# First edge sums of a graph kernel: one-hots two groups ahead among the additions, weighted one-hots that wait piece by piece, four message buffers

## The chip, the cores and the metric

One Trainium2 chip, one NeuronCore. The metric is the device time of one launch, in microseconds (us). The kernel before is timed in three runs, and one further run is profiled. In the rows PE is TensorE's matmul, PEld its weight load, DVE VectorE, ACT ScalarE, POOL GpSimd, SP SyncE; a q behind an engine's name is its instruction queue (register work, reads into registers, DMA issue).

## The reference, cut to what matters

The kernel computes two layers of a graph model over 3125 nodes of 256 features and 50,000 edges that are sorted by destination: layer norm, graph attention, a transformer mixer of four sublayers, a mixture of experts, then a second layer of the same kind. The change touches one step of the first graph attention. Each edge has a message of 64 features and four attention scores; per destination node and head the messages are summed with weight exp(score), the weights themselves are summed, and the edges are counted for the second layer:

```
exp_scores = jnp.exp(scores - scores.max(axis=0, keepdims=True))
sum_exp = jax.ops.segment_sum(exp_scores, dst, num_segments=N)
norm = exp_scores / (sum_exp[dst] + 1e-10)
outs = [jax.ops.segment_sum(messages * norm[:, hd:hd + 1], dst, num_segments=N) for hd in range(H)]
deg = jax.ops.segment_sum(jnp.ones_like(src, dtype=x.dtype), dst, num_segments=n)
```

## The kernel before, in words

The program runs in stages, with a barrier of all engines between two of them (`stage_end`). Stage 2 makes the messages beside the mixer and spills them to HBM (`spill`). Stage 3, the first edge sums, is where the change lies; stage 4 turns the sums (line 1583) and goes on to the experts.

Stage 3 works in 40 groups (`NCG`) of 10 chunks (`CG`) of 128 edges. Two chunks share a window of 48 nodes (`W`), so a group has 5 windows (`PR`). A group goes through the engines so:

- SP loads the group's messages from `spill` into `msg` (lines 826 and 835), one of two buffers, 340 KB; load n waits until PE has ended group n - 2 (`win_ps`). Behind the first two loads it issues the 3 MB of `xin` (line 828).
- DVE makes the one-hots: it compares each edge's node number within the window with an iota (line 3027, `one_hots`) and writes `ohd`, one of two buffers.
- POOL multiplies the one-hots by the weights of three heads in two pieces, of 4 and 6 chunks (line 1054, `weigh_hots`), into `ohx`, one of two buffers. It then writes the column of ones into the messages (line 1040, `ones_column`), and after 25 of the 40 groups adds one tile of `xin` to `z` (line 1065). Before its second weighing POOL waits for all of `xin`. ACT makes the product of the fourth head, chunk by chunk (line 2187).
- PE waits for the column of ones (`msg_one`), sums the degrees from `ohd` (line 1562, bank `pt`), and then for each window multiplies messages by weighted one-hots into one of five banks (line 1565, `pa` and `pb`). A window waits for its weighing piece (`wm_ready`), its ACT products (`ax_ready`), and for DVE to have added the same window of the group before (`win_used`).
- DVE reads the five start positions of the group's windows into registers (line 3033, `window_starts`), then adds each window into `acc` (line 3043) and its degrees (line 3049), `add_windows`. An addition waits for its product and for the addition before it, since windows may overlap.

The order on DVE's queue is written out in the loop: the one-hots of group n + 1, the register read of group n, the five additions of group n.

```
for n in range(NCG):
    if n + 1 < NCG:
        one_hots(n + 1)
    ...
    add_windows(n, window_starts(n))
```

A semaphore that is used up by one stage is used again under another name by a later one; the table `past` (line 595 on) holds the value from which it then counts. `mhalf` is a small constant that POOL's powers use.

Of the kernel before, what the change touches and what calls it, by code (L numbers as in the profile page):

```python
# [25 lines left out]
P = 128  # L26
# [83 lines left out]
MSG_HEAD = 4  # L110
MSG_SLOT = (3, 4, 4, 4, 4)
# [47 lines left out]
def build(nc, ctx, a, out):  # L159
# [44 lines left out]
    hn = sb("hn", [TP, GT, D])  # L204
    s0 = ExitStack()
# [94 lines left out]
    msg = sb("msg", [P, 2, CG, MW], F32, s3)  # L300
# [54 lines left out]
    mhalf = sb("mhalf", [TP, GT], F32, s5)  # L355
# [236 lines left out]
    for new, old, value in (("e_ld0", "wq_ld", 128), ("e_ld1", "bo_ld", 128), ("e_ld2", "wvo_ld", 128), ("e_ld3", "sm_ld", 320),  # L592
# [5 lines left out]
                            ("yo_go", "m_add", 3 * NG * NL), ("uw_ld0", "msg_st0", 16 * NCG), ("uw_ld1", "msg_st1", 16 * NCG), ("uw_ld2", "msg_ld0", 8 * NCG), ("yo_st0", "w1_ld", 48), ("yo_st1", "w2_ld", 64),  # L598
# [114 lines left out]
    def _(sp):  # L713
# [111 lines left out]
        for b in range(2):  # L825
            sp.dma_start(msg[:, b].rearrange("p c f -> p (c f)"), spill[b]).then_inc(s[f"msg_ld{b}"], 16)
# [5 lines left out]
        with sp.Fori(1, NCG // 2) as i:  # L832
            for b in range(2):
                sp.wait_ge(s["win_ps"], (i * 2 + b - 1) * PR)
                sp.dma_start(msg[:, b].rearrange("p c f -> p (c f)"),
                             spill[bass.ds(i * 2 + b, 1)].rearrange("o p c -> p (o c)")).then_inc(s[f"msg_ld{b}"], 16)
# [102 lines left out]
    def _(pool):  # L939
# [97 lines left out]
        def ones_column(n):  # L1037

            pool.wait_ge(s[f"msg_ld{n % 2}"], 16 * (n // 2) + 16)
            nc.gpsimd.memset(msg[:, n % 2, :, MF:MF + 1], 1.0).then_inc(s["msg_one"], 1)  # L1040
# [5 lines left out]
        def weigh_hots(n):  # L1046
# [4 lines left out]
            for at in (slice(0, 4), slice(4, CG)):  # L1051
                cols = slice(n * CG + at.start, n * CG + at.stop)
# [5 lines left out]
        for n in range(NCG):  # L1058
            weigh_hots(n)
            if n >= 2:  # L1060
                ones_column(n)
# [109 lines left out]
    def _(pe):  # L1171
# [377 lines left out]
        for n in range(NCG):  # L1549
            b = n % 2  # L1550
            pe.wait_ge(s["msg_one"], n + 1)
            for q in range(PR):
# [11 lines left out]
                for c in (2 * q, 2 * q + 1):  # L1564
                    last = nc.tensor.matmul(wbank[q][0:MF + 1, 0:MH * W], msg[:, b, c, 0:MF + 1],
                                            ohx[:, b, c].rearrange("p k w -> p (k w)"), start=c == 2 * q, stop=c == 2 * q + 1)
# [388 lines left out]
    def _(act):  # L1955
# [226 lines left out]
        for n in range(NCG):  # L2182
            b = n % 2
            act.wait_ge(s["oh_ready"], n + 1)
            for q in range(PR):
                for c in (2 * q, 2 * q + 1):
# [201 lines left out]
    def _(dve):  # L2388
# [648 lines left out]
        def add_windows(n, starts):  # L3037

            for q, at in enumerate(starts):
# [9 lines left out]
                nc.vector.tensor_tensor(degrees, degrees, pt[0:MF + 1, n % 2, q * W:(q + 1) * W], ALU.add).then_inc(s["deg_used"], 1)  # L3049

        me.link(dve, nc.vector.tensor_copy(ohd_one[:, :], ones[:, 0:MF + 1]))
        one_hots(0)
        for n in range(NCG):
            if n + 1 < NCG:
                one_hots(n + 1)
# [671 lines left out]
```

## Time and profile before

| | us |
|---|---|
| median of three runs (lowest to highest) | 2686.23 (2679.67 to 2689.53) |
| the profiled execution's own time | 2686.39 |
| span of the profiled execution | 2684.7 |
| stage 3, first one-hots to last addition | 1256.0 to 1431.2 |
| mean granted TensorE clock over the span | 0.937 |

The span goes from the first to the last instruction; the own time has some 1.7 us more around it. A row of a timeline has the start in us, the duration in us, the engine, the line and the operation, what is written and what it is made from, and in square brackets the idle time before it with what ended it. Merged rows have a count (x12), and their duration runs from the first start to the last end. A row of one line's instructions has durations in ns as lowest/median/highest, and then the start of the first and of the last.

### The profile page before, as it was taken

How to read it: one execution, taken by the hardware profiler on the slowest of the kernel's cores; microseconds unless marked ns; L12 is line 12 of the kernel's file. 1: busy time of each engine (PE TensorE's matmuls, PEld its weight loads, DVE VectorE, ACT ScalarE, POOL GpSimd, SP SyncE). 2: the span in 40 equal slices, each digit the busy share in tenths (PEclk: the TensorE clock that was granted, in tenths of full speed). 3: DMA queues.
4: the chain of work that ended last, by engine and by line, in shares of the span. 5: the costliest groups of instructions: out<-in, count | busy, mean ns of one | idle time of the engine just before them, and what ended most of it. 6: DMA issues, size and time to landing. Idle time of an engine off the chain costs nothing. (4 is left out here: it accounts for less than half of the span.)

```text
span 2684.7 us, 46904 instructions
## 1 busy us (share of the span) xinstructions
PE 2418.1 (90%) x16106; PEld 2259.9 (84%) x16106; DVE 1758.2 (65%) x4475; ACT 1353.8 (50%) x2913; POOL 1239.0 (46%) x1402
## 2 busy tenths in 40 slices
PE   7888999899988998997999699966888999999998
PEld 6778998799988997997778588855777899998998
DVE  6666777678768776765776523246876677677565
ACT  4334655555545664555553222233333366665687
POOL 1323454244515552565886222245777377776000
PEclk9989999999999999999996699977999599999899
DMA  5211112111121111124233354536666077775011
GB/s 115 71 40 39 39 42 64 45 41 41 44 66 38 43 47 49 44 58 103 84 90 98 98 170 143 142 116 178 196 202 189 14 213 206 218 216 174 24 36 32
DMA packets 150287, 259.77 MB, mean 97 GB/s; under 512 B 35713, under 2 KB 95884, under 8 KB 149926
## 3 DMA queue, kind: packets, MB, share of 16 engines
q0 software_dynamic: 49632, 145.61, 20.5%
q1 hardware_dynamic: 100422, 111.17, 13.9%
q8 instruction: 132, 2.16, 0.3%
q14 instruction: 101, 0.83, 0.1%
HBM read 219.88 MB, written 36.82 MB: 96 GB/s over the span
## 5 line engine op out<-in xcount | busy, mean ns | idle before, releaser
L976 POOL DMA_INDIRECT gat<-table,srcT x400 | 413.0, 1032 | 351.8 <-DVE m L2829 228.8
L1131 POOL DMA_INDIRECT x_rows<-table,srcT x392 | 397.3, 1014 | 184.1 <-issue 120.6
L633 PE MATMUL pa<-w,act 128*125 128x256 f32 x2400 | 357.9, 287 | 13.1 <-DVE act L2588 12.9
L633 PE MATMUL pb<-hT,w 128*128 128x378 f32 (+1 forms) x1920 | 335.8, 311 | 1.8 <-DVE hT L2664 1.0
L633 PEld LDWEIGHTS pa<-w,act 128*125 128x125 f32 x2400 | 313.4, 187 | 17.9 <-DVE act L2588 17.9
L633 PEld LDWEIGHTS pb<-hT,w 128*128 128x128 f32 x1920 | 286.4, 189 | 4.1 <-DVE hT L2664 1.8
L2287 ACT ACTIVATE gf<-pb,bne 128x378 f32<-128x378 f32 (+1 forms) x320 | 194.2, 607 | 157.6 <-PE pb L633 145.7
L2588 DVE TENSOR_TENSOR act<-gf,act 128x378 fp32r<-128x378 f32 (+1 forms) x320 | 153.9, 484 | 106.8 <-ACT act L2005 105.0
L2002 ACT ACTIVATE gf<-pb,b1s 128x378 f32<-128x378 f32 (+1 forms) x320 | 165.9, 518 | 107.8 <-PE pb L633 97.0
L633 PE MATMUL pb<-xT,fw 128*128 128x378 f32 (+1 forms) x960 | 158.8, 316 | 0.0
L2220 ACT ACTIVATE hid<-pb,b1u 128x256 f32<-128x256 f32 x128 | 60.7, 474 | 187.8 <-PE pb L1651 187.8
L2005 ACT ACTIVATE act<-gf 128x378 fp32r<-128x378 f32 (+1 forms) x320 | 149.8, 468 | 10.2
L3570 DVE TENSOR_TENSOR act<-gf,act 128x378 fp32r<-128x378 f32 (+1 forms) x180 | 87.9, 489 | 101.5 <-ACT act L2291 101.0
L633 PE MATMUL pb<-act,fw 128*128 128x378 f32 (+1 forms) x960 | 153.8, 309 | 0.0
L1097 POOL DMA_INDIRECT xtok<-table,tabi x64 | 61.4, 960 | 193.1 <-PE pt L1640 142.7
L633 PEld LDWEIGHTS pb<-xT,fw 128*128 128x128 f32 x960 | 146.2, 196 | 1.4 <-issue 1.3
L633 PEld LDWEIGHTS pb<-act,fw 128*128 128x128 f32 x960 | 142.1, 190 | 0.0
L1651 PE MATMUL pb<-xtT,e 128*128 128x256 f32 x512 | 133.6, 384 | 3.8 <-issue 2.2
L2187 ACT ACTIVATE ohx<-ohd,ex 128x48 f32<-128x48 f32 x400 | 94.4, 320 | 74.5 <-DVE ohd L3027 74.5
L1739 PE MATMUL pg<-x_rows,oh 128*125 128x256 f32 x632 | 105.4, 294 | 28.5 <-DMA x_rows<-table,srcT 18.5
L1054 POOL TENSOR_TENSOR ohx<-ohd,ex 128x576 f32<-128x576 f32 x80 | 110.3, 1399 | 40.1 <-DVE ohd L3027 29.0
L1739 PEld LDWEIGHTS pg<-x_rows,oh 128*125 128x125 f32 x632 | 86.6, 190 | 40.1 <-DMA x_rows<-table,srcT 18.9
(517 smaller groups left out, 5676.4 us busy)
## 6 DMA issues: line engine op xcount, KB each, us to landing
e<-in_L_ffn_W_dram SPq DMA_DIRECT2D x40, 512.0 KB, 4.4
spill<-m SPq DMA_DIRECT2D x80, 170.0 KB
msg<-spill SPq DMA_DIRECT2D x40, 340.0 KB, 2.9
yslots<-yo SPq DMA_DIRECT2D x64, 128.0 KB, 2.0
fraw<-in_L_ffn_W_dram SPq DMA_DIRECT2D x32, 256.0 KB
w1r<-in_L_mix_W_dram SPq DMA_DIRECT2D x7, 1024.0 KB, 4.9
gat<-table,srcT POOLq DMA_INDIRECT x400
x_rows<-table,srcT POOLq DMA_INDIRECT x392, 3.8
```

The lines of the kernel that those rows point to most:

```text
L633: mm = nc.tensor.matmul(ps, lhs(l), rhs(r), start=first and n == 0, stop=last and n == 2)
L976: pool.indirect_dma_start(out=gat[:, i % 2, c, :], out_offset=None, in_=table0, in_offset=bass.IndirectOffsetOnAxis(ap=srcT[:, i * GC + c: ...
L1054: nc.gpsimd.tensor_tensor(ohx[:, n % 2, at, 0:MH - 1, :], ohd[:, n % 2, at, :].bitcast(F32).unsqueeze(2).to_broadcast([P, k, MH - 1, W]), ...
L1131: pool.indirect_dma_start(out=x_rows[:, n % UB, c, :].bitcast(F32), out_offset=None, in_=table1, in_offset=bass.IndirectOffsetOnAxis(ap=sr ...
L1651: last = nc.tensor.matmul(pb[:, f % 2, 0:UT], e1[:, u % 3, k, f * P:(f + 1) * P], xtT[:, u % 2, k, :], start=k == 0, stop=k == H - 1)
L1739: last = nc.tensor.matmul(to, oh1[:, n % UB, c, :], x_rows[:, n % UB, c, k * D:(k + 1) * D], start=c == 0 and k == 0, stop=c == UG - 1 and ...
L2002: nc.scalar.activation(gf[:, f % 2, 0:n], pb[:, f % 2, 0:n], func, bias=bias, scale=scale).then_inc(s["gf_done"], 1)
L2005: nc.scalar.activation(act_[0][:, f % 4, 0:n], gf[:, f % 2, 0:n], ACT.Copy).then_inc(s["f_hi"], 1)
L2187: last = nc.scalar.mul(ohx[:, b, c, MH - 1, :], ohd[:, b, c, :].bitcast(F32), ex[:, n * CG + c, MH - 1:MH])
L2287: nc.scalar.activation(gf[:, f % 2, 0:n], pb[:, f % 2, 0:n], func, bias=bias, scale=scale).then_inc(s["gf_done"], 1)
L2588: nc.vector.tensor_tensor(act_[1][:, f % 4, 0:n], gf[:, f % 2, 0:n], act_[0][:, f % 4, 0:n], ALU.subtract).then_inc(s["f_lo"], 1)
L3570: nc.vector.tensor_tensor(to[1][:, f, 0:n], gf[:, f, 0:n], to[0][:, f, 0:n], ALU.subtract).then_inc(s["f_lo"], 1)
```

## The change

It makes the one-hots of groups 0 and 1 ahead of the loop, and those of group n + 2 inside `add_windows(n)`, behind the second of the five additions, after two waits on POOL's and ACT's work of groups up to n. The weighing pieces on POOL and the ACT products of group n wait for PE's products of group n - 2, which read the same `ohx` buffer: the first piece for two windows, the second for all five, ACT window by window. `msg` has four buffers in place of two; load n waits for the end of group n - 4, and POOL writes the column of ones of group n + 2 behind its weighing of group n. The four first message loads stand ahead of `xin` in SP's queue. `mhalf` leaves the memory that the larger `msg` takes. The numbers of semaphores that are used again follow.

```diff
--- before.py
+++ after.py
@@ -108,6 +108,7 @@
 PAIRS = ((0, 2), (2, 1), (3, 2))
 RING = (0, 1, 2, 0, 1)
 MSG_HEAD = 4
+MSG_RING = 4
 MSG_SLOT = (3, 4, 4, 4, 4)
 UC = 2
 UG = RR
@@ -202,6 +203,7 @@
     si = sb("si", [P, 2 * NT], I32)
     r7 = sb("r7", [TP, 3, NT])
     hn = sb("hn", [TP, GT, D])
+    mhalf = sb("mhalf", [TP, GT])
     s0 = ExitStack()
     bns = sb("bns", [P, NE, 4, H], F32, s0)
     bne = sb("bne", [P, 2, 4, H], F32, s0)
@@ -297,7 +299,7 @@
     s3 = ExitStack()
     xin = sb("xin", [TP, NT, D], F32, s3)
     ex = sb("ex", [P, NCH, MH], F32, s3)
-    msg = sb("msg", [P, 2, CG, MW], F32, s3)
+    msg = sb("msg", [P, MSG_RING, CG, MW], F32, s3)
     ohx = sb("ohx", [P, 2, CG, MH, W], F32, s3)
     ohd = sb("ohd", [P, 2, CG, W], R32, s3)
     ohd_one = sb("ohd_one", [P, MF + 1], R32, s3)
@@ -352,7 +354,6 @@
     cr = sb("cr", [P, H], F32, s5)
     qm = sb("qm", [TP, GT * AH], F32, s5)
     qr = sb("qr", [TP, GT * AH], F32, s5)
-    mhalf = sb("mhalf", [TP, GT], F32, s5)
     n_bn, h_bn = [sb(f"{k}_bn", [TP, GT, 6], F32, s5) for k in "nh"]
     n_mv, h_mv = [sb(f"{k}_mv", [TP, GT, 2], F32, s5) for k in "nh"]
     n_ve, h_ve = [sb(f"{k}_ve", [TP, GT], F32, s5) for k in "nh"]
@@ -595,7 +596,8 @@
                             ("z_add", "tn_T", NL), ("z_ve", "cx_ps", NL), ("z_nr", "cx_go", NL), ("hot_w", "bq_ps", NL), ("b1_go", "bq_ev", NL), ("deg_used", "mo_ps", NL),
                             ("tab_go", "tn_go", NL), ("acc1_0", "ta_go", NL), ("xg_ld0", "gat0", 16 * GC * NCG), ("xg_ld1", "gat1", 16 * GC * NCG),
                             ("xg_T", "n_T", 3 * NG * NL), ("xg_up", "n_hi", 3 * NG * NL),
-                            ("yo_go", "m_add", 3 * NG * NL), ("uw_ld0", "msg_st0", 16 * NCG), ("uw_ld1", "msg_st1", 16 * NCG), ("uw_ld2", "msg_ld0", 8 * NCG), ("yo_st0", "w1_ld", 48), ("yo_st1", "w2_ld", 64),
+                            ("yo_go", "m_add", 3 * NG * NL), ("uw_ld0", "msg_st0", 16 * NCG), ("uw_ld1", "msg_st1", 16 * NCG), ("uw_ld2", "msg_ld0", 4 * NCG), ("msg_ld2", "w1_ld", 48), ("msg_ld3", "w2_ld", 64),
+                            ("yo_st0", "w1_ld", 48 + 4 * NCG), ("yo_st1", "w2_ld", 64 + 4 * NCG),
                             ("rw5", "gat0", 16 * GC * NCG + 16 * NUN), ("rw6", "gat1", 16 * GC * NCG + 16 * NUN), ("ch_used", "bc_ps", NL * NG),
                             ("cg_ld0", "rw0", 0), ("cg_ld1", "rw1", 0), ("cg_ld2", "rw2", 0), ("cg_ld3", "rw3", 0),
                             ("cg_used", "d_add", GT * NL * NG), ("tr_hi", "q_hi", 3 * NG * NL)):
@@ -822,18 +824,18 @@
             sp.wait_ge(s[f"msg_st{b}"], 16 * NCG)
         stage_end(sp, 2)
 
-        for b in range(2):
+        for b in range(MSG_RING):
             sp.dma_start(msg[:, b].rearrange("p c f -> p (c f)"), spill[b]).then_inc(s[f"msg_ld{b}"], 16)
         for to, of in by_rows(xin[:, :, :], a["x"].rearrange("(t p) d -> p t d", p=TP)):
             sp.dma_start(to, of).then_inc(s["xin_ld"], 16)
         sp.dma_start(gw6[:, :, :], a["L0_ffn_gate_w"].rearrange("(h p) e -> p h e", p=P)).then_inc(s["p6_ld"], 16)
         sp.dma_start(lgb6[:, :], a["L0_ffn_gate_b"].rearrange("(o e) -> o e", o=1).to_broadcast([TP, NE])).then_inc(s["p6_ld"], 16)
 
-        with sp.Fori(1, NCG // 2) as i:
-            for b in range(2):
-                sp.wait_ge(s["win_ps"], (i * 2 + b - 1) * PR)
+        with sp.Fori(1, NCG // MSG_RING) as i:
+            for b in range(MSG_RING):
+                sp.wait_ge(s["win_ps"], (i * MSG_RING + (b - MSG_RING + 1)) * PR)
                 sp.dma_start(msg[:, b].rearrange("p c f -> p (c f)"),
-                             spill[bass.ds(i * 2 + b, 1)].rearrange("o p c -> p (o c)")).then_inc(s[f"msg_ld{b}"], 16)
+                             spill[bass.ds(i * MSG_RING + b, 1)].rearrange("o p c -> p (o c)")).then_inc(s[f"msg_ld{b}"], 16)
         with sp.If(rest_flag(sp) == 1):
             sp.wait_ge(s["win_ps"], NPR)
             with sp.Fori(0, NCG) as n:
@@ -1036,8 +1038,9 @@
 
         def ones_column(n):
 
-            pool.wait_ge(s[f"msg_ld{n % 2}"], 16 * (n // 2) + 16)
-            nc.gpsimd.memset(msg[:, n % 2, :, MF:MF + 1], 1.0).then_inc(s["msg_one"], 1)
+            b = n % MSG_RING
+            pool.wait_ge(s[f"msg_ld{b}"], past.get(f"msg_ld{b}", 0) + 16 * (n // MSG_RING + 1))
+            nc.gpsimd.memset(msg[:, b, :, MF:MF + 1], 1.0).then_inc(s["msg_one"], 1)
 
         nc.gpsimd.memset(acc[:, 0:2, :], 0.0).then_inc(s["const"], 1)
         ones_column(0)
@@ -1049,6 +1052,8 @@
                 pool.wait_ge(s["act_go"], 1 + MH)
             pool.wait_ge(s["oh_ready"], n + 1)
             for at in (slice(0, 4), slice(4, CG)):
+                if n >= 2:
+                    pool.wait_ge(s["win_ps"], (n - 2) * PR + at.stop // 2)
                 cols = slice(n * CG + at.start, n * CG + at.stop)
                 k = at.stop - at.start
                 nc.gpsimd.tensor_tensor(ohx[:, n % 2, at, 0:MH - 1, :], ohd[:, n % 2, at, :].bitcast(F32).unsqueeze(2).to_broadcast([P, k, MH - 1, W]),
@@ -1057,8 +1062,8 @@
 
         for n in range(NCG):
             weigh_hots(n)
-            if n >= 2:
-                ones_column(n)
+            if n + 2 < NCG:
+                ones_column(n + 2)
             if n == 0:
                 pool.wait_ge(s["xin_ld"], 32)
             for t in range(n * NT // NCG, (n + 1) * NT // NCG):
@@ -1562,7 +1567,7 @@
                         nc.tensor.matmul(pt[0:MF + 1, b, 0:PR * W].rearrange("p (q w) -> p q w", q=PR), ohd_one[:, :], hots[:, :, k, :],
                                          start=k == 0, stop=k == 1)
                 for c in (2 * q, 2 * q + 1):
-                    last = nc.tensor.matmul(wbank[q][0:MF + 1, 0:MH * W], msg[:, b, c, 0:MF + 1],
+                    last = nc.tensor.matmul(wbank[q][0:MF + 1, 0:MH * W], msg[:, n % MSG_RING, c, 0:MF + 1],
                                             ohx[:, b, c].rearrange("p k w -> p (k w)"), start=c == 2 * q, stop=c == 2 * q + 1)
                 last.then_inc(s["win_ps"], 1)
         with pe.If(rest_flag(pe) == 1):
@@ -2183,6 +2188,8 @@
             b = n % 2
             act.wait_ge(s["oh_ready"], n + 1)
             for q in range(PR):
+                if n >= 2:
+                    act.wait_ge(s["win_ps"], (n - 2) * PR + q + 1)
                 for c in (2 * q, 2 * q + 1):
                     last = nc.scalar.mul(ohx[:, b, c, MH - 1, :], ohd[:, b, c, :].bitcast(F32), ex[:, n * CG + c, MH - 1:MH])
                 last.then_inc(s["ax_ready"], 1)
@@ -3047,12 +3054,15 @@
                     dve.wait_ge(s["deg_used"], past["deg_used"] + n * PR + q)
                 degrees = acc[:, MH:MH + 1, bass.ds(at, W)].rearrange("p o n -> p (o n)")
                 nc.vector.tensor_tensor(degrees, degrees, pt[0:MF + 1, n % 2, q * W:(q + 1) * W], ALU.add).then_inc(s["deg_used"], 1)
+                if q == 1 and n + 2 < NCG:
+                    dve.wait_ge(s["wm_ready"], 2 * (n + 1))
+                    dve.wait_ge(s["ax_ready"], (n + 1) * PR)
+                    one_hots(n + 2)
 
         me.link(dve, nc.vector.tensor_copy(ohd_one[:, :], ones[:, 0:MF + 1]))
         one_hots(0)
+        one_hots(1)
         for n in range(NCG):
-            if n + 1 < NCG:
-                one_hots(n + 1)
             if n == 0:
                 me.link(dve, nc.vector.memset(acc[:, 2:MH, :], 0.0))
                 dve.wait_ge(s["const"], 4)
```

## Rows read from the trace of the kernel before

**Rows 1.** The page: busy time and share of the span, instructions, of each engine.

```profile
PE 2418.1 (90%) x16106; PEld 2259.9 (84%) x16106; DVE 1758.2 (65%) x4475; ACT 1353.8 (50%) x2913; POOL 1239.0 (46%) x1402
```

**Rows 2.** Busy time of each engine in the stage's steady part, then clock, DMA share, GB/s.

```profile
1280.00:1431.00 151.00, 138.22 (x826) 108.33 (x824) 111.41 (x415) 87.24 (x370) 122.00 (x141) 1.00 0.30 86
```

**Rows 3.** Timeline of one group, DVE.

```profile
1342.62 0.35 DVE L3043 TENSOR_TENSOR acc<-acc,pb 65x192 f32 x1
...
1342.89 0.19 DVE L3049 TENSOR_TENSOR acc<-acc,pt 65x48 f32 x1
...
1343.01 0.65 DVE L3027 TENSOR_TENSOR ohd<-iota,relT 128x480 fp32r<-128x480 f32 x1
...
1344.23 0.35 DVE L3043 TENSOR_TENSOR acc<-acc,pa 65x192 f32 x1 [0.57 <-PE pa L1565]
...
1344.79 0.35 DVE L3043 TENSOR_TENSOR acc<-acc,pa 65x192 f32 x1
...
1346.58 0.35 DVE L3043 TENSOR_TENSOR acc<-acc,pb 65x192 f32 x1 [0.18 <-PE pb L1565]
```

**Rows 4.** Timeline of the same group, weight loads and POOL.

```profile
1341.01 1.64 POOL L1054 TENSOR_TENSOR ohx<-ohd,ex 128x864 f32<-128x864 f32 x1
...
1342.75 0.19 PEld L1562 LDWEIGHTS pt<-ohd,ohd_one 128*65 128x65 f32 x2 [0.73 <-POOL msg L1040]
...
1343.73 2.75 POOL L1054 TENSOR_TENSOR ohx<-ohd,ex 128x576 f32<-128x576 f32 x2 [1.03 <-DVE ohd L3027]
...
1344.82 1.27 PEld L1565 LDWEIGHTS pb<-ohx,msg 128*65 128x65 f32 x8
...
1346.49 0.72 POOL L1065 TENSOR_TENSOR z<-z,xin 125x256 f32<-125x256 f32 x1
...
1346.59 0.19 PEld L1562 LDWEIGHTS pt<-ohd,ohd_one 128*65 128x65 f32 x2 [0.50 <-POOL msg L1040]
```

**Rows 5.** The comparison's line, and the register read's line twice, four groups each.

```profile
L3027 DVE TENSOR_TENSOR ohd<-iota,relT x37: 645/648/993, 1279.1 to 1423.0; 128x480 fp32r<-128x480 f32 x37
...
L3033 DVEq TENSOR_LOAD <-base_i x4: 593/1184/1187, 1334.9 to 1346.8; - x4
...
L3033 DVEq TENSOR_LOAD <-base_i x4: 597/1180/1190, 1350.6 to 1362.9; - x4
```

**Rows 6.** Timelines of DVE and POOL at two places where both are busy.

```profile
1299.06 1.43 POOL L1065 TENSOR_TENSOR z<-z,xin 125x256 f32<-125x256 f32 x1
...
1350.56 0.73 POOL L1065 TENSOR_TENSOR z<-z,xin 125x256 f32<-125x256 f32 x1
...
1350.81 0.99 DVE L3027 TENSOR_TENSOR ohd<-iota,relT 128x480 fp32r<-128x480 f32 x1
```

**Rows 7.** Start and end of the stage: one stretch's busy time and GB/s, then timelines.

```profile
1256.00:1266.00 10.00, 4.88 (x29) 3.79 (x28) 7.55 (x7) 5.75 (x22) 3.09 (x4) 0.96 1.11 241
...
1251.34 6.55 SPq L828 DMA_DIRECT2D xin<-in_x_dram  x2
...
1262.27 0.38 SPq L835 DMA_DIRECT2D msg<-spill  x1
...
1271.02 2.75 POOL L1054 TENSOR_TENSOR ohx<-ohd,ex 128x576 f32<-128x576 f32 x2 [11.16 <-DMA xin<-in_x_dram]
...
1275.62 0.35 DVE L3043 TENSOR_TENSOR acc<-acc,pa 65x192 f32 x1 [0.81 <-PE pa L1565]
...
1280.46 0.35 DVE L3043 TENSOR_TENSOR acc<-acc,pa 65x192 f32 x1 [0.69 <-PE pa L1565]
...
1428.01 0.35 DVE L3043 TENSOR_TENSOR acc<-acc,pa 65x192 f32 x1 [1.10 <-PE pa L1565]
...
1430.75 0.35 DVE L3043 TENSOR_TENSOR acc<-acc,pb 65x192 f32 x1 [0.54 <-PE pb L1565]
```

**Rows 8.** The message loads' landing times, and one column of ones that waited for one.

```profile
DMA to landing us min/median/max: 2.7/2.9/4.2
...
1299.00 0.12 POOL L1040 MEMSET msg<- 128x10 f32 x1 [0.46 <-DMA msg<-spill]
```

## The prediction, as recorded before the run

> **What bounds the kernel now.** I read the page first: TensorE is busy for nine tenths of the span [rows 1]. That average hides the stage that the change touches: the forty groups of the first edge sums run from 1256 to 1431 us, 175 us or 6.5% of the span. The busy time by stretch shows their steady part [rows 2], where no engine is full: PE 92%, POOL 81%, DVE 74%. Nothing else of the program changes its work, so the answer lies in those 175 us.
>
> The one-hot comparisons, one a group, give the pace: 37 of them from 1279.1 to 1423.0 us, 36 periods of 4.00 us [rows 5]. What sets it is a loop over two groups, read from the timeline of one group [rows 3, 4]. PE starts group n at 1342.75 and DVE begins to add its fifth window at 1346.58: 3.83 us. From a fifth addition to the comparison of the group after next is 0.39 (1342.62 to 1343.01), from there to the weighing on POOL 0.72, the two weighing pieces take 2.75, and PE starts 0.11 after them, once POOL has written the column of ones. 7.80 us for two groups is 3.90 each; some groups add a POOL or PE delay, and 4.00 is measured. PE itself would allow less: its loads of a group begin at 1342.75 and end at 1344.82 + 1.27 = 1346.09, 3.34 us. This gap of 0.66 us a group, 26 us over the stage, is the most that the change can win.
>
> The other row to see is DVE's own chain. From a fifth addition (1342.62) to the next group's first (1344.23) are 1.61 us. Most of that is not the comparison but the read of the five window starts into registers, which DVE's queue does before it can issue the first addition: 1.18 us in three groups of four, 0.59 in the fourth [rows 5]. The comparison of 0.65 us runs inside this read. Additions then follow each other by 0.56 (1344.23 to 1344.79). So DVE alone needs 1.61 + 4 x 0.557 = 3.84 us with a long read and 3.25 with a short one: it is only just inside the 4.00.
>
> **The change part by part.**
>
> *One-hots two groups ahead, among the additions.* The loop above falls: a group's comparison no longer waits for the fifth addition and its weighing has over a group's time to spare. In the code the comparison now stands behind the second addition, while the register read stays where it was, alone. Its cover is gone. A comparison there costs DVE: 0.27 from an addition to its degree addition (1342.62 to 1342.89), 0.12 to the comparison (to 1343.01), then 0.65 less the 0.08 by which neighbours on DVE overlap (0.35 - 0.27), so 0.96 from the second to the third addition in place of 0.56. That is 0.40 us a group, exposed. The two waits ahead of it (weights and ScalarE's products of the group before) ask for work finished a group earlier, and cost at most a slot in the queue. No row shows a comparison between additions: the lower bound is 0, if it slid into slack as under the read now; the upper is its whole 0.65. I take 0.40, by the overlap in the neighbouring rows. A group is then 1.61 + 3 x 0.557 + 0.96 = 4.24 us with a long read, 3.65 with a short one.
>
> *Does PE still hold DVE up?* It has five banks and can be five windows ahead; 3.34 is below 3.65, so it gets ahead and waits for banks. Every addition then finds its product done, and I count 0.56 for each.
>
> *Weighings that wait piece by piece.* POOL waits for the products of the group two before (two of them, then all five), ScalarE pair by pair. With PE ahead of DVE these are done before the comparison is even made. POOL starts 0.72 after the comparison starts, ends the weighings at 3.47, and in 25 of 40 groups adds z until 3.48 + 0.72 = 4.20.
>
> *That addition against the comparison.* At 1350.56 POOL added z for 0.73 us; the comparison that began at 1350.81 took 0.99 in place of 0.65, and ended as if it had started at 1351.15, 0.14 before the z record's end. The other way round, the z addition at 1299.06, over which a comparison ran, took 1.43 [rows 6]. One waits for the other. So DVE's next comparison can't start before 4.20 - 0.13 = 4.07. A long period (4.24) clears this; a short one (3.65) is held by 0.42 where z is added, in 4 of the 9 short groups: 1.7 us.
>
> The Trainium skill, "SBUF — State Buffer", section "SBUF: two separate sides", states that a DVE operation with two SBUF inputs and a GpSimd operation that reads SBUF take a shared port pair as a lock for the whole instruction. The rows agree; by their times, the lock goes 0.14 us before the end that the record shows. Held to the record's very end it would add 0.13 in those four groups, 0.5 us.
>
> *Four message buffers.* The column of ones is written a group and more ahead, so PE no longer waits for it. A later load is issued when PE ends the group four before and lands in 2.9 us [rows 8]; POOL wants it some 4.5 us after that. It costs nothing. But two more loads of 340 KB now stand ahead of xin in SP's queue, and POOL's second weighing waits for xin: 11.16 us idle until 1271.02 [rows 7]. At the 241 GB/s of that stretch 0.68 MB are 2.8 us; one load of 0.34 MB, issued at 1262.27 and so in competition with the later part of xin, is no longer there, at most 1.4 back. Bounds 1.4 and 2.8; I take 1.8, as that load shared most of the tail.
>
> *Start, worked out.* Weighing 1 runs from 1272.8 to 1275.6, z to 1276.3, weighing 2 to 1279.1. Comparison 3 is asked for 0.39 after group 1's second addition (1275.62 + 1.8), at 1277.8, falls on the longer weighing piece and waits until 1279.0. The fifth addition of group 1 comes at 1279.0 + 0.57 + 2 x 0.56 = 1280.7, group 2's first at 1282.3 to 1282.4, in place of 1280.46 [rows 7]: +1.9.
>
> *mhalf* moves to another address and does the same work. No wait hangs on it: 0.
>
> **Sum.** Group 2's first addition to group 39's: before 1428.01 - 1280.46 = 147.55 us. After: 37 periods, 28 long and 9 short, 28 x 4.24 + 9 x 3.65 = 151.6, less 0.4 for group 38, which makes no comparison, plus 1.7 for the lock: 152.9, +5.3. Last group: four steps of 0.56 in place of 2.74 (1428.01 to 1430.75), -0.5. With the start (+1.9): +6.7. The profiled execution took 2686.4 us (its span 2684.7), so 2693.1; the median of the runs, 0.2 lower, gives 2692.9: I predict 2693.0. The expected gain is given back by DVE, which becomes the bound.
>
> **Rivals.** (a) *PE becomes the bound*: the period falls to 3.34, and 37 x 0.65 = 24 us go; with start and end 2663.6. It needs both the register read and the comparison to leave DVE's path. Against it: the read occupies the queue that must issue the additions, and each addition waits for the one before. 0.12. (b) *The comparison costs DVE nothing*: 0.40 x 36 = 14.4 less, 2678.6. PE and POOL would allow it. Against it: DVE has no idle time left there. 0.10. (c) *Slower, by POOL*: if PE doesn't get ahead, it ends a group only as DVE adds its fifth window, 1.5 us after the comparison's start; the load that waits for this lands at 4.5, POOL's column of ones, due at 3.4, is held, and the z addition behind it runs to 5.3 and locks out the comparison until 5.2. One us in each of 23 groups: 2716. It decides once POOL's z addition is over 0.17 us late; some 0.5 late makes +7, enough to be slower. For it: one memset waited 0.46 for its load even now [rows 8]. Against it: PE's 3.34. 0.18. Against the weighing piece of 1.64 us [rows 4] the comparison could be held in the same way; that needs POOL to be 0.9 us late (4.24 less 3.47, plus 0.13). The Trainium skill's rule on the port pair, named above, states no exception for such a pair.
>
> **How the numbers follow.** What a measurement of this kernel can tell from no change is about 0.5%, 13.4 us. The forecast has 0.60; its own range, comparison 0.2 to 0.6 exposed (-7, +7) and the start, is 2685 to 2702, and 0.08 of it lies above 2699.6. (b) is nearly all within, (a) is faster, (c) slower. Faster 0.14, same 0.60, slower 0.26. The range takes in (b) and the lower half of (c): 2670 to 2708.
>
> **What would show it.** Right: the register reads still take 1.18 and 0.59 us and now stand without a comparison behind them; second to third addition 0.96; fifth to first 1.6; additions never wait for PE; ScalarE and POOL idle for DVE's comparison; PE idle for a DVE bank; comparisons 4.1 apart. Wrong: a period below 3.7 (the read was not on the path), comparisons of over 1 us in many groups (the lock, case c), or PE at the lower clock in mid-stage.

## The result, and the profile after

| | before | after |
|---|---|---|
| median of the runs beside each other, us | 2683.23 (20 runs, 2678.08 to 2693.08) | 2697.84 (20 runs, 2683.67 to 2702.66) |
| ratio, 95% interval | | 1.0037 (1.0026 to 1.0049) |
| profiled execution: time, span, us | 2686.4, 2684.7 | 2700.5, 2698.7 |
| mean granted clock | 0.937 | 0.928 |
| the stage, first comparison to last addition's end, us | 1256.02 to 1431.21: 175.19 | 1257.02 to 1440.36: 183.34 |
| first comparison to group 2's first addition, us | 24.44 | 26.82 |
| group 2's first addition to group 39's, us (per group) | 147.54 (3.99) | 153.82 (4.16) |
| group 39's first addition to its fifth, us | 2.74 | 2.23 |

The ratio makes 9.9 us (7 to 13) of 2683: slightly slower, by less than the 0.5% that the prediction counts as a change. The two medians lie further apart, by 14.6, the means of the 20 runs by 10.5 (2684.5 and 2695.1). The runs of each kernel scatter by 15 to 19, so I hold the parts against the ratio. The stage grew by 8.15 us, which lies inside that interval: 2.4 at the start, 6.3 in the steady part, 0.5 back in the last group. The stage's times come from one profiled execution of each kernel. A second one of the changed kernel, on another chip (e9 below), has 182.32 in place of 183.34: 0.7 less at the start, 0.3 less in the steady part.

The page of the changed kernel, each engine's busy time, share and instructions, beside [rows 1]:

```profile
PE 2423.6 (90%) x16106; PEld 2263.7 (84%) x16106; DVE 1755.6 (65%) x4475; ACT 1352.5 (50%) x2913; POOL 1239.5 (46%) x1402
```

The same work, and sums that moved by 6 us at most: the page doesn't show the change. Nor does the busy time by stretch of the steady part (stretch, length, then PE, PEld, DVE, ACT, POOL, granted clock, DMA share, GB/s), beside [rows 2]:

```profile
1280.00:1435.00 155.00, 138.63 (x828) 108.55 (x827) 107.04 (x408) 87.42 (x370) 120.83 (x139) 1.00 0.28 80
```

DVE is shown busy for 107.04 of 155.00 us, 69%, less than PE and POOL, and yet it sets the pace. One has to read the timeline of its groups. Here are groups 17 and 18 (start, duration, engine, line, operation, tiles; in brackets the idle time before it and what ended it):

```profile
1346.26 0.35 DVE L3050 TENSOR_TENSOR acc<-acc,pa 65x192 f32 x1 [1.11 <-PE pb L1570]
1346.53 0.19 DVE L3056 TENSOR_TENSOR acc<-acc,pt 65x48 f32 x1
1346.81 0.35 DVE L3050 TENSOR_TENSOR acc<-acc,pa 65x192 f32 x1
1347.08 0.19 DVE L3056 TENSOR_TENSOR acc<-acc,pt 65x48 f32 x1
1347.20 0.65 DVE L3034 TENSOR_TENSOR ohd<-iota,relT 128x480 fp32r<-128x480 f32 x1
1347.77 0.34 DVE L3050 TENSOR_TENSOR acc<-acc,pa 65x192 f32 x1
...
1348.88 0.35 DVE L3050 TENSOR_TENSOR acc<-acc,pb 65x192 f32 x1
...
1350.45 0.35 DVE L3050 TENSOR_TENSOR acc<-acc,pa 65x192 f32 x1 [1.11 <-PE pb L1570]
```

From the second addition to the third are 0.96 us, with the comparison between them; from the fifth to the next group's first 1.57. The idle time of 1.11 is put down to PE's product, but that is not what ended it. It is the register read, which the profile keeps on DVE's queue. The waits of 1290 to 1435 us (engine, line, waited for: us in total, times, longest) and the two lines, read and comparison (duration in ns min/median/max, first and last start), over the whole stage:

```profile
ACT ohx L2194 <- DVE ohd L3034: 63.0, 35, 2.2
...
POOL ohx L1059 <- DVE ohd L3034: 32.0, 35, 1.8
...
PE pt L1567 <- DVE acc L3056: 15.3, 26, 0.9
```
```profile
L3040 DVEq TENSOR_LOAD <-base_i x40: 590/1182/1200, 1265.0 to 1436.3; - x40
...
L3034 DVE TENSOR_TENSOR ohd<-iota,relT x40: 647/648/1716, 1257.0 to 1430.5; 128x480 fp32r<-128x480 f32 x40
```

ACT and POOL wait for the comparison, and PE waits for DVE to free a bank, where it used to wait for POOL [rows 4]: all three are now held by DVE. The same in the timelines of PE and POOL around group 18:

```profile
1351.05 0.41 PE L1567 MATMUL pt<-ohd,ohd_one 128*65 128x240 f32 x2 [0.54 <-DVE acc L3056]
```
```profile
1347.93 2.75 POOL L1059 TENSOR_TENSOR ohx<-ohd,ex 128x576 f32<-128x576 f32 x2 [1.39 <-DVE ohd L3034]
1350.62 0.12 POOL L1043 MEMSET msg<- 128x10 f32 x1
1350.67 0.72 POOL L1070 TENSOR_TENSOR z<-z,xin 125x256 f32<-125x256 f32 x1
```

**The start.** xin stands behind two more loads:

```profile
1253.28 8.43 SPq L830 DMA_DIRECT2D xin<-in_x_dram  x2
...
1274.38 2.75 POOL L1059 TENSOR_TENSOR ohx<-ohd,ex 128x576 f32<-128x576 f32 x2 [13.47 <-DMA xin<-in_x_dram]
...
1279.36 1.72 DVE L3034 TENSOR_TENSOR ohd<-iota,relT 128x480 fp32r<-128x480 f32 x1
...
1283.84 0.35 DVE L3050 TENSOR_TENSOR acc<-acc,pa 65x192 f32 x1 [1.11 <-PE pa L1570]
```

From the first comparison to POOL's release by xin were 15.00 us (1271.02 less 1256.02) and are 17.36. Comparison 3 falls on a weighing piece and takes 1.72. How far the start varies from execution to execution is seen in the table below: with four loads ahead of xin it takes 25.99 to 28.68 us (after, e1 to e4, e9, e11), with two 23.44 to 24.77 (before, e7, e8). The longer start is clear of this scatter, its size of 2.4 is not fixed to better than 1 us.

**Behind the stage.** From the last addition's end to the first transposition were 1.09 us and are 1.50. The granted clock fell from the higher of its two levels to the lower near there in both kernels: before, 3.0 us behind the last addition (at 1434.2), after, 1.2 behind it (at 1441.6). The first transpositions, before and after, in the columns of the stretch above:

```profile
1432.25:1433.70 1.45, 1.40 (x13) 1.40 (x13) 0.43 (x4) 0.00 (x0) 0.00 (x0) 1.00 0.12 33
```
```profile
1441.80:1443.40 1.60, 1.54 (x8) 1.54 (x8) 0.08 (x1) 0.00 (x0) 0.00 (x0) 0.50 0.31 35
```

Before, 13 of them still ran at clock 1.00 (2.4 GHz); after, all eight of that stretch ran at 0.50 (1.2 GHz). The trace of after runs 9.15 us behind that of before at the last addition's end (1.00 from ahead of the stage, 8.15 from it) and 10.8 behind by the sixteenth transposition. These 1.6 us did not last. Some 130 us later the same products ran at the lower level before and at the higher one after:

```profile
1565.00:1567.00 2.00, 2.00 (x6) 1.55 (x6) 0.85 (x2) 0.03 (x1) 0.00 (x0) 0.50 0.75 280
```
```profile
1575.00:1577.00 2.00, 2.00 (x11) 1.77 (x10) 0.85 (x2) 0.47 (x1) 0.00 (x0) 1.00 0.91 322
```

Behind them the traces lie 8.4 apart, less than at the stage's end. The spans end 14.0 apart, so the rest came in later stages, in two executions of kernels whose runs scatter by 15 to 19. What the traces show of the change for certain is the stage's 8.15; the 9.9 of the ratio, with 7 to 13, agrees with that and needs nothing more.

### The profile page after: what moved, and what is told of

It reads as the page before. It is cut to its first block and busy times, and to the rows that moved or that the text cites. A ratio compares the mean times of both kernels' runs of the same rounds, so it can differ in the third digit from the quotient of the medians.

```text
span 2698.7 us, 46992 instructions
## 1 busy us (share of the span) xinstructions
PE 2423.6 (90%) x16106; PEld 2263.7 (84%) x16106; DVE 1755.6 (65%) x4475; ACT 1352.5 (50%) x2913; POOL 1239.5 (46%) x1402
```

## The experiments

All ratios are against the kernel before on the same chip. e1 to e4 and e5 to e8 ran on two chips on which it takes 2809 and 2810 us, e9 and e10, then e11 and e12, on two where it takes 2688 and 2689. Of the difference some 17 us lie ahead of the stage and some 97 behind it (e1's trace against that of after). The stage's own times agree where a kernel ran on both kinds of chip (e6 151.45, e12 151.63), so I compare those. Each is from one profiled execution. "Steady" is group 2's first addition to group 39's; "start" the first comparison to group 2's first addition.

| kernel | whole, us | ratio (95%) | stage | start | steady (pace) |
|---|---|---|---|---|---|
| before | 2683.23 | | 175.19 | 24.44 | 147.54 (3.99) |
| after | 2697.84 | 1.0037 | 183.34 | 26.82 | 153.82 (4.16) |
| e1 comparison under the read | 2805.87 | 0.9999 (0.9974 to 1.0025) | 171.79 | 27.26 | 141.84 (3.83) |
| e2 short reads | 2805.07 | 1.0008 (0.9984 to 1.0032) | 169.57 | 26.27 | 140.60 (3.80) |
| e3 both | 2802.86 | 0.9993 (0.9963 to 1.0023) | 163.01 | 25.99 | 134.18 (3.63) |
| e4 both, no z | 2771.6 | one run | 159.42 | 28.46 | 128.00 (3.46) |
| e5 both, z late | 2792.55 | 0.9940 (0.9919 to 0.9961) | 156.51 | 15.99 | 137.67 (3.72) |
| e6 both, z late on DVE | 2787.87 | 0.9923 (0.9896 to 0.9950) | 151.45 | 15.95 | 132.80 (3.59) |
| e7 xin first | 2822.0 | one run | 180.74 | 24.77 | 153.27 (4.14) |
| e8 before, short reads | 2811.36 | one run | 174.07 | 23.44 | 147.30 (3.98) |
| e9 = after again | 2703.92 | one run | 182.32 | 26.10 | 153.52 (4.15) |
| e10 after, z late | 2686.75 | 1.0003 (0.9983 to 1.0024) | 175.16 | 17.50 | 154.96 (4.19) |
| e11 reads twice | 2742.95 | one run | 221.92 | 28.68 | 190.55 (5.15) |
| e12 = e6 | 2665.39 | 0.9910 (0.9888 to 0.9932) | 151.63 | 16.05 | 132.89 (3.59) |

**e1: the comparison back under the read.** In the changed kernel, the comparison behind the fifth addition:

```diff
-                if q == 1 and n + 2 < NCG:
+                if q == PR - 1 and n + 2 < NCG:
```

> The changed kernel with one edit: the one-hots of group n + 2 stand behind the fifth addition, so ahead of the next register read, and no longer behind the second. Theory (DVE's queue sets the pace, and the comparison costs 0.40 us because it lost the read as its cover): second to third addition 0.56 in place of 0.96, fifth to first still 1.57 to 1.61 with a long read. DVE alone would then allow 3.84 (long) and 3.25 (short), 3.70 on average; POOL and the comparison, which wait for each other, need 4.07 in groups with a z addition and 3.35 in the others, 3.80 on average, so some 3.8 a group against 4.16 measured: 12 to 14 us less than the changed kernel, 2 to 4 less than the kernel before. Rival (the pace of the changed kernel comes from the waits piece by piece or from the lock, not from where the comparison stands): the place makes no difference, within 3 us of the changed kernel.

The steady part is 12.0 us shorter than after (12 to 14 were expected), the stage 11.6. DVE's timeline from a fifth addition:

```profile
1356.99 0.35 DVE L3050 TENSOR_TENSOR acc<-acc,pb 65x192 f32 x1
1357.26 0.20 DVE L3056 TENSOR_TENSOR acc<-acc,pt 65x48 f32 x1
1357.38 0.68 DVE L3034 TENSOR_TENSOR ohd<-iota,relT 128x480 fp32r<-128x480 f32 x1
1358.67 0.35 DVE L3050 TENSOR_TENSOR acc<-acc,pa 65x192 f32 x1 [0.61 <-PE pa L1570]
```

Fifth to first is 1.68, 0.11 more than after: the read starts 0.28 behind the fifth addition, where it was 0.17, and in the queue the comparison's waits now stand ahead of it. Against it stand the 0.40 of the comparison that is no longer exposed. Groups take 3.91 with a long read, 3.32 with a short one. So the place of the comparison is what turns a gain into a loss: with it under the read the same change shortens the stage by 3.4 us. Over the whole kernel so little can't be seen (ratio 0.9999).

**e2: short reads.** The window starts are copied once into rows of eight, and each group reads from there:

```diff
+    base_8 = sb("base_8", [1, NCG * 8], I32, s3)
+        me.link(dve, nc.vector.tensor_copy(base_8[:, :].rearrange("o (n k) -> o n k", k=8)[:, :, 0:PR],
+                                           base_i[:, :].rearrange("o (n k) -> o n k", k=PR)))
-                base_i[0:1, n * PR:(n + 1) * PR], engines=[mybir.EngineType.DVE]
+                base_8[0:1, n * 8:n * 8 + PR], engines=[mybir.EngineType.DVE]
```

> The changed kernel with the window starts copied once into rows of eight, so that each group's five lie at a multiple of 32 bytes. Theory (the register read is on DVE's path, and is long where its start is not at a multiple of 16 bytes): all 40 reads take 0.59 us, fifth to first addition 0.98 in every group. DVE's period falls to 3.60; where POOL adds z the comparison is held until 4.07, in 25 of 40 groups, so 3.89 on average: some 10 us less than the changed kernel, and comparisons of 1.1 us in the z groups. Rival 1 (the read is hidden by something else): no change. Rival 2 (the lock does not hold DVE in general): 3.60, 20 us less.

The read's line, in the form of the one above:

```profile
L3041 DVEq TENSOR_LOAD <-base x38: 584/587/591, 1300.5 to 1441.1; - x38
```

Every read is short, fifth to first is 0.98 in all groups but two (1.33), and the steady part is 13.2 us shorter than after, more than the 10 expected. Part of what the read gave is taken by POOL's work, which holds the comparison: from group 2 on 21 of 36 comparisons take 0.79 us or more. Eleven are held by a z addition, and the worst of those make a group of 4.07, which is the bound that the prediction gave for this; ten are held by a weighing, for 0.2 us, mostly in groups of 3.82. Unheld groups take 3.60. The expectation had 25 groups at 4.07 and so too small a gain.

**e8: short reads in the kernel before.** The counterpart, which a theory of the read alone would have faster:

> The kernel before with short register reads alone. Theory (before the change a loop over two groups set the pace, PE's products, the comparison, POOL's weighings, and the read lay beside it): the pace stays at 3.9 to 4.0 us a group, at most 3 us less over the stage. Rival (the read was on the path before too): 0.4 to 0.6 less a group, 15 to 20 us.

Its steady part is 147.30 in place of 147.54. The same 0.6 us that are worth 0.36 a group after are worth nothing before: DVE's chain did not set the pace there. That fits the two-group loop.

**e11: reads used twice.** In the changed kernel each group reads its five values twice, and the second set places the degree additions:

```diff
-            add_windows(n, window_starts(n))
+            add_windows(n, window_starts(n), window_starts(n))
```

> The changed kernel with a second register read per group, whose values place the degree additions, so that both reads are needed (the kernel with a read whose values nothing used had 40 reads in its trace, as many as the changed kernel: it was the changed kernel again). Theory (the read is serial on DVE's queue): fifth to first addition 1.57 + 1.18 = 2.75 with a long read, 0.98 + 0.59 = 1.57 with a short one; 38 us more from group 2 to group 39 than the 154 of the changed kernel, less up to 2 where the longer group frees the comparison from the lock. Rival (part of it overlaps with waiting that would be there anyway): less than 25 us more.

```profile
L3040 DVEq TENSOR_LOAD <-base_i x8: 595/1181/1192, 1351.5 to 1368.1; - x8
...
1351.34 0.35 DVE L3050 TENSOR_TENSOR acc<-acc,pb 65x192 f32 x1
...
1354.12 0.35 DVE L3050 TENSOR_TENSOR acc<-acc,pa 65x192 f32 x1 [2.32 <-issue]
```

The steady part grows by 36.7 us. Fifth to first is 2.79 in a long group (2.78 in the one shown, over 3.1 in two), and 1.60 in a short one. The read is on the path in full.

**e9** was to show the same with a second read whose values nothing used. Only 40 reads stood in its trace, so it was the changed kernel again and tells nothing of the read. It does repeat the changed kernel on another chip: stage 182.32, pace 4.15.

> The changed kernel with each group's register read issued twice. Theory (the read is serial on DVE's queue): fifth to first addition 1.57 + 1.18 = 2.75 with a long read, 0.98 + 0.59 = 1.57 with a short one, 28 x 1.18 + 9 x 0.59 = 38 us more from group 2 to group 39, a pace of 5.2 us. Rival (part of the read overlaps with waiting that would be there anyway): less than 25 us more.

**e3: both.** e1 and e2 together.

> Both edits, comparison under the read and short reads. Theory: DVE alone 3.25, PE 3.34, but POOL with the comparison 3.80 on average, so about the time of the kernel with the comparison under the read alone, 13 us less than the changed kernel: the bound has moved to POOL. Rival (DVE's chain alone sets the pace): 3.34 to 3.4, PE's own pace, 28 us less.

3.63 a group is neither of the two. The comparison's line, then DVE's and POOL's timelines:

```profile
L3035 DVE TENSOR_TENSOR ohd<-iota,relT x37: 646/1133/1284, 1298.8 to 1429.6; 128x480 fp32r<-128x480 f32 x37
...
1342.13 0.82 DVE L3035 TENSOR_TENSOR ohd<-iota,relT 128x480 fp32r<-128x480 f32 x1
```
```profile
1339.68 2.75 POOL L1060 TENSOR_TENSOR ohx<-ohd,ex 128x576 f32<-128x576 f32 x2 [0.54 <-DVE ohd L3035]
...
1342.43 1.10 POOL L1071 TENSOR_TENSOR z<-z,xin 125x256 f32<-125x256 f32 x1
1343.49 2.75 POOL L1060 TENSOR_TENSOR ohx<-ohd,ex 128x576 f32<-128x576 f32 x2
```

The comparison, asked for at 1342.13, is held by the weighing and ends at 1342.95. It goes ahead of the z addition, which stands next on POOL and then takes 1.10 in place of 0.72. So the operations exclude each other one by one, and their times add up: weighings 2.7, comparison 0.65 and what z adds, 0.45, make 3.8 (groups with z take 3.81); without z it is 3.35, as measured. The 0.45 is z's 1.10 less the comparison's 0.65, so it is read from the same rows and no independent test; alone the z addition has a record of 0.72. The expectation took the 0.72 and came to 3.80 on average, where 25 groups of 3.81 and 15 of 3.35 make 3.64. That is the rule of the Trainium skill, "SBUF — State Buffer", section "SBUF: two separate sides": DVE operations with two SBUF inputs and GpSimd operations that read SBUF share a port pair, one instruction at a time. The rows agree. Here it is the pace of the stage, where in the changed kernel it cost 2.5 us of the steady part.

**e4: both, without the z additions.** It leaves out the addition of the input x to z, 25 instructions.

> Both edits, and the 25 additions of x to z on POOL in this stage left out (so z lacks that term). Theory (POOL's z additions lock the comparison out and fill POOL): the period falls from 3.8 to PE's own pace, 3.34 to 3.45, no comparison longer than 0.65 us: the stage some 15 us shorter than with both edits. Rival (something else holds the stage, for instance the column of ones or the landing of messages): it stays at 3.8.

```profile
L3033 DVE TENSOR_TENSOR ohd<-iota,relT x37: 645/648/682, 1298.3 to 1423.0; 128x480 fp32r<-128x480 f32 x37
```

No comparison is held any more. The steady part gives 6.2 us, not 15, since with z it was already below the 3.80 on which that was reckoned. What sets the pace of 3.46 is PE. Over 1310 to 1420 us this trace shows no wait of PE, and DVE waits for PE's products 38 times (waits of that stretch; then two groups' first products, and the 12 behind the first of them):

```profile
DVE acc L3049 <- PE pb L1569: 7.1, 38, 0.5
```
```profile
1349.29 0.52 PE L1566 MATMUL pt<-ohd,ohd_one 128*65 128x240 f32 x2
1349.64 2.11 PE L1569 MATMUL pa<-ohx,msg 128*65 128x192 f32 x12
...
1352.76 0.52 PE L1566 MATMUL pt<-ohd,ohd_one 128*65 128x240 f32 x2
```

A group takes PE 3.47 us when nothing holds it: its 20 products start 0.162 apart (2.11 less the last one's 0.33, over 11), 3.2 in all, and the two products for the degrees make the rest. The prediction's 3.34 went from the first weight load to the end of the last and left out the time until the next group's first load. From comparison to weighing and the weighings (0.73 + 2.74) are 3.47 too, but POOL stands idle for 0.66 of it, until the comparison, which comes 0.39 behind a fifth addition that had waited for PE. Of this kernel only the stage is compared: with a term of z left out the later stages work on other numbers.

**e7: xin first.** In the changed kernel, message loads 2 and 3 stand behind xin, and POOL writes the column of ones of group n + 1 behind the weighing of n:

```diff
-        for b in range(MSG_RING):
+        for b in range(2):
...
+        for b in range(2, MSG_RING):
```

> The changed kernel with the third and fourth message load behind xin in SP's queue, and the column of ones of group n + 1 behind the weighing of group n. Theory (two more loads ahead of xin made the start 2.4 us longer): from the first comparison to group 2's first addition 24.4 us as before the change, in place of 26.8; the steady pace 4.16 unchanged. Rival (the start is longer because the comparison of group 3 is held by a weighing): it stays over 26.

The start is 24.77, 2.05 less than after and 0.33 more than before. That the two loads are what made it longer is clear; the split is not, since two executions of the changed kernel differ by 0.7 (26.82 and 26.10) and before and e8, with the same loads, by 1.0. The comparison is held for 1.72 here as after, and may be the 0.33. The steady part is 153.27, 0.55 less than after, 0.36 of it in group 3, whose comparison isn't held here.

**e5: both, z late.** The start's real cost is POOL's wait for xin, so the wait and the z additions move to groups 8 to 39:

```diff
-            if n == 0:
+            if n < 8:
+                continue
+            if n == 8:
                 pool.wait_ge(s["xin_ld"], 32)
-            for t in range(n * NT // NCG, (n + 1) * NT // NCG):
+            for t in range((n - 8) * NT // 32, (n - 7) * NT // 32):
```

> Both edits (comparison under the read, short reads), and POOL's wait for xin with the 25 additions to z moved from groups 0 to 39 into groups 8 to 39. Theory (the stall at the start is POOL's wait for xin ahead of its second weighing, and nothing else needs xin so early): PE starts group 1 within some 5 us of group 0, PE's clock does not fall between them, the first addition of group 2 comes 12 us earlier, and the steady pace stays at the 3.63 measured with both edits. Stage 151 us; some 20 us (0.7%) less than the kernel before. Rival (DVE's work at the start, the clearing of the sums and the first reads, or the first loads, hold group 1 anyway): under 5 us from the start.

The start falls by 10.0 us against e3, where 12 were expected, and the granted clock does fall there, to 0.83 over 1285 to 1295. The steady part rises by 3.5 where no change was expected, 2.3 of it once, in group 3: the column of ones of a message buffer waits 4.0 us for a load that was issued behind xin. So the stage is 156.5, not 151.

```profile
1290.70 2.75 POOL L1060 TENSOR_TENSOR ohx<-ohd,ex 128x576 f32<-128x576 f32 x2 [5.64 <-DVE ohd L3037]
1297.49 0.12 POOL L1044 MEMSET msg<- 128x10 f32 x1 [4.04 <-DMA msg<-spill]
```

**e10: z late in the changed kernel alone.**

> The changed kernel with POOL's wait for xin and the 25 z additions moved from groups 0 to 39 into groups 8 to 39, nothing else. Theory (the start is one cost, DVE's chain another, and they add up): the first addition of group 2 comes 10 us earlier than in the changed kernel, as with both edits, and the pace stays 4.1 to 4.2; stage 173 us, the whole 0.1 to 0.4% less than the kernel before. Rival (without the stall POOL or the loads fall behind): the pace rises above 4.3.

The start gives 9.3 us, the pace is 4.19 (4.16 after), and the stage is 175.16, as long as before the change and 2 more than expected; the whole ratio is 1.0003. So in the stage this step is worth its 8 us by itself, and the DVE chain stays what it is.

**e6 and e12: both, z late and on DVE.** The z additions go from POOL to DVE, behind the comparison:

```diff
                     one_hots(n + 2)
+                if q == PR - 1 and n >= 8:
+                    if n == 8:
+                        dve.wait_ge(s["xin_ld"], 32)
+                    for t in range((n - 8) * NT // 32, (n - 7) * NT // 32):
+                        me(nc.vector.tensor_tensor(z[:, t, :], z[:, t, :], xin[:, t, :], ALU.add))
```

> As the kernel with both edits and late z additions, but the z additions on DVE, behind the comparison, in place of POOL. Theory (POOL's weighings and the comparison exclude each other: 3.47 without z on POOL; a z addition on DVE reads two operands from SBUF and excludes POOL in the same way, for 0.4 us): 3.47 in groups without and 3.8 in groups with a z addition, 3.7 on average, no better than on POOL. Rival (only POOL's time counts): 3.47 throughout, 5 us less.

> The same kernel as e6, once more, beside the kernel before. Theory: the stage is 151 to 152 us as in e6, 23 to 24 less than before the change, which is 0.9% of the whole: ratio 0.990 to 0.993. Rival (much of e6's gain over the whole was scatter of the later stages): ratio over 0.995.

e12's comparison line and one group of its DVE timeline:

```profile
L3031 DVE TENSOR_TENSOR ohd<-iota,relT x35: 646/648/684, 1284.2 to 1403.6; 128x480 fp32r<-128x480 f32 x35
...
1343.65 0.35 DVE L3047 TENSOR_TENSOR acc<-acc,pb 65x192 f32 x1
...
1344.04 0.65 DVE L3031 TENSOR_TENSOR ohd<-iota,relT 128x480 fp32r<-128x480 f32 x1
1344.61 0.41 DVE L3062 TENSOR_TENSOR z<-z,xin 125x256 f32<-125x256 f32 x1
1344.94 0.34 DVE L3047 TENSOR_TENSOR acc<-acc,pa 65x192 f32 x1
```

e6's steady part is 4.9 us shorter than e5's, so the theory (no better than on POOL) failed and the rival had the size. On DVE the same addition takes 0.41 and adds 0.2 to fifth to first (1.29 in place of 1.09, as from 1347.16 to 1348.25 in a group without one): comparison and addition together have the read of 0.59 beside them. A group with one takes 3.52, one without 3.31. No comparison in the row above is held. From group 4 on e12 goes at 3.51 a group, close to PE's own 3.47. The stage takes 151.5 us on both chips, and the whole kernel 0.9910 (0.9888 to 0.9932) and 0.9923 of before: 24 and 22 us less, in line with the 23.6 of the stage. It beats both kernels.

What I leave open: e3's stage is 12.2 us shorter, 0.43% of its chip's 2809, and its whole time is 0.07% shorter with an interval that ends at 0.37%. e2's stage is 5.6 us shorter, 0.20%, and its interval ends at 0.16%. Some of the stage's gain did not reach the end in either, and no run shows where it went. Both comparisons set the stage against the one trace of before, which comes from another chip.

## Why the prediction was right

The time, 2697.8, lies 4.8 above the 2693.0 and in the range: the medians are 14.6 apart where 6.8 was predicted, and before's came out 3.0 lower than in the three runs shown. The likeliest case, no difference over 0.5%, came. The ratio's 9.9 is 3.2 more than the sum's 6.7, the stage's own 8.15 is 1.4 more, and that is the better test, since the prediction is a sum over the stage. By its steps:

- **What bounded it before** was not DVE's chain. e8 shows it: reads shorter by 0.6 us changed the steady part by 0.2. That it was the loop over two groups rests on the prediction's rows; e1 fits it (with the comparison under the read in both, opening the loop gave 5.7 us of the steady part).
- **The comparison among the additions, 0.40 exposed**: second to third addition is 0.95 to 0.96 in place of 0.56. Right, and e1 takes it away again.
- **The read on the path**: predicted 1.61 and 1.02 from fifth to first, measured 1.57 and 0.98. A group takes 4.19 and 3.60, predicted 4.24 and 3.65. The 0.04 come off because no comparison runs ahead of the read. e2 and e11 show the read's whole length on the path, from either side.
- **The lock**: predicted 0.42 in each of 4 groups. Groups 8, 16, 24 and 32 had second to third 1.42, 0.47 more. The comparisons of groups 3 and 21, long ones, were held by a z addition too, for 0.36 and 0.23; 2.5 us in all where 1.7 were predicted. One of the four:

```profile
1308.99 0.35 DVE L3050 TENSOR_TENSOR acc<-acc,pa 65x192 f32 x1
...
1309.37 1.11 DVE L3034 TENSOR_TENSOR ohd<-iota,relT 128x480 fp32r<-128x480 f32 x1
...
1310.41 0.34 DVE L3050 TENSOR_TENSOR acc<-acc,pa 65x192 f32 x1
```
```profile
1309.25 0.72 POOL L1070 TENSOR_TENSOR z<-z,xin 125x256 f32<-125x256 f32 x1
```

  As in the prediction's rows, the comparison goes on before the record of z ends: its last 0.65 begin at 1309.83, and z's record ends at 1309.97.
- **Steady part, +5.3**: measured +6.3, since 28 x 4.19 + 9 x 3.60 + 1.9 = 151.6, and eight single delays add 2.4 between them (0.14 to 0.37 each, in groups 3, 6, 10, 19, 21, 24, 29 and 33), less 0.2 for group 38. Those in groups 3 and 21 are the lock. The other six, 1.8 us, were a term that the sum put at nothing; they stand in the same groups with the same sizes in e7 and e9, so they are no scatter, but their cause stays open.
- **Start, +1.9**: measured +2.4 in one execution, +1.7 in another (e9). Both predicted parts are there, the two loads (e7: 2.05, inside the bounds of 1.4 to 2.8) and comparison 3 held by a weighing; with a scatter of 0.7 to 1.0 neither is shown to be mis-sized.
- **Last group, -0.5**: measured 2.23 in place of 2.74.
- **PE's own pace, 3.34**: wrong by 0.13. e4 shows 3.47, with PE waiting for nothing, so the most that the change could win was 0.5 a group (3.99 less 3.47), 19 us in place of 26, and rival (a) was priced too high. The forecast doesn't hang on it, as 3.47 is still below the 3.65 of a short group.
- **Behind the stage** the sum has nothing. The 1.6 us shown there were gone some 130 us later, so they explain none of the 9.9. That the median, 2697.8, lies 11.6 above the 2686.2 from which the forecast starts is more than the stage explains; the rest is within the scatter of the runs.

Of the rivals, (a), PE as the bound, did not come. It needed three things gone, not the two that were named: with the comparison under the read and the read short, POOL and the comparison set the pace (e3: 3.63), and only without the z additions did PE (e4: 3.46, at its own 3.47). (b), the comparison at no cost, is refuted by the 0.96. (c), POOL late, did not happen: over 1290 to 1435 POOL waited for a load once, 0.3 us.

```profile
POOL msg L1043 <- DMA msg<-spill: 0.3, 1, 0.3
```

Its mechanism, the comparison locked out by POOL's work, is nevertheless what holds e3, once DVE is fast enough to meet it.

## What to carry to other kernels

Work that is moved "ahead" on an engine has to be priced at its new place. Here a loop over two groups was opened at the price of taking 0.65 us of work out from under a register read that has to be waited for anyway; in the old place the same change would have shortened the stage. Look at the queue's own instructions (register reads, waits) when an engine that is 70% busy seems to be the bound, and ask of each resource two engines share whether their times add up to the period you hope for.

## What the runs showed of the hardware, unexpectedly

- A register read of five int32 values takes 0.59 us or 1.18, depending on where the row starts. With rows of five, one in four is short (starts at multiples of 80 bytes); with rows of eight, starts at multiples of 32 bytes, all 38 were short (584 to 591 ns). That the start's alignment decides is read from these two layouts alone; the 16 bytes that e2's expectation names fit both, and no run tests that limit by itself.
- A read whose values nothing uses isn't in the trace at all (e9: 40 reads, not 80).
- On the shared port the waiting DVE operation goes ahead of POOL's next one even where POOL's queue has it ready (e3's comparison at 1342.13 ahead of the z addition at 1342.43), so a short DVE operation waits for one GpSimd instruction, not for a run of them.
- The same 125x256 addition takes 0.72 us on POOL and 0.41 on DVE, and moving it brought the groups that have one from 3.81 us (e3) to 3.52 (e6).
- The granted clock fell near the stage's end in both kernels, 3.0 and 1.2 us behind the last addition; where it fell against the work decided whether 13 transpositions or none ran at the higher level. The 1.6 us lost there came back where the clock stood at 1.00 after and 0.50 before, so a difference at one place of two traces isn't yet a difference of the kernels.
- 20 products of 128x65 by 128x192 in fp32 follow each other by 0.162 us, and with the two for the degrees a group takes PE 3.47 us (e4), 0.13 more than from its first weight load to the end of its last.
